# Attention steps of a two-layer block laid out anew: who holds which PSUM bank, and which engine splits what

## What is computed

```
h = layernorm(x) * (1 + ca) + sa
x = x + ga * attention_1(h)      # 32 heads of 64, 8 key heads, rotary, a window of 128, sinks
h = layernorm(x) * (1 + cb) + sb
x = x + gb * block_2(h)          # h + causal attention of rmsnorm(h), then a top-2 mixture of 8 experts
```

## Time and profile before

| | us |
|---|---|
| runs: median (lowest to highest, 3) | 1406.89 (1406.08 to 1414.29) |
| profiled execution, whole | 1400.63 |
| its span, first to last instruction | 1398.7 |
| TensorE busy in the span | 1064.0 (76%) |
| VectorE | 792.3 (57%) |
| ScalarE | 712.4 (51%) |
| GpSimd | 478.8 (34%) |

### The profile page before, as it was taken

One profiled execution on the slowest core, in us unless ns is written; L12 is line 12 of the kernel. 1 busy time (PEld: TensorE's weight loads), 2 busy tenths in 40 slices (PEclk: granted clock), 3 DMA queues, 4 the chain that ended last, 5 costly groups with the idle time before them and its releaser, 6 DMA issues.

```text
span 1398.7 us, 22967 instructions
## 1 busy us (share of the span) xinstructions
PE 1064.0 (76%) x6836; PEld 946.2 (68%) x6836; DVE 792.3 (57%) x2276; ACT 712.4 (51%) x2003; POOL 478.8 (34%) x659
## 2 busy tenths in 40 slices
PE   3647767777775677779878999988899726889893
PEld 1336666667665566668767888877788616888883
DVE  4445565555555554456655666656666553666655
ACT  2124535455453454566665666675676523555541
POOL 2355544755653454244222424322222140000003
PEclk7778978999997798999999999999999957999997
DMA  6455445545731343454344345534332063555513
GB/s 144 124 121 166 129 128 140 164 131 163 168 93 46 98 123 96 132 135 142 89 123 99 99 121 135 145 84 128 84 88 49 1 227 105 155 144 151 151 39 104
DMA packets 151823, 166.58 MB, mean 119 GB/s; under 512 B 79572, under 2 KB 108180, under 8 KB 146580
## 3 DMA queue, kind: packets, MB, share of 16 engines
q1 hardware_dynamic: 129427, 143.27, 38.8%
q10 hardware_dynamic: 20736, 17.64, 3.9%
q0 software_dynamic: 1536, 4.20, 0.9%
HBM read 106.28 MB, written 58.79 MB: 118 GB/s over the span
## 4 chain that ended last, share of the span: by engine, by line
PE 37%; issue 8%; DVE 6%; ACT 4%; DMA 3%; POOL 2%; ACTq 1%; SPq 0%; DVEq 0%; POOLq 0%
PE psO L917 7%; PE psS L882 5%; PE psX L892 4%; PE psP L817 4%; PE psS L1075 3%; PE psX L1075 3%; PE psY L933 3%; DMA kd<-st 2%; PE psO L1096 2%; PE psP L1096 2%; ACT pTh L1136 1%; DVE pbuf L1481 1%; PE psP L900 1%; DVE pTl L1497 1%; POOL xg L766 1%
## 5 line engine op out<-in xcount | busy, mean ns | idle before, releaser
L1167 ACT ACTIVATE pbuf<-pbuf,nmax 128x256 f32<-128x256 f32 (+3 forms) x512 | 265.5, 519 | 298.0 <-DVE nmax L1481 296.7
L1481 DVE CUSTOM_DVE_ANT_0 pbuf<-psS,mcau 128x256 f32<-128x256 f32 (+3 forms) x512 | 215.4, 437 | 55.8 <-PE psS L882 52.4
L1497 DVE TENSOR_TENSOR pTl<-psX,pTh 128x512 fp32r<-128x512 f32 x272 | 187.5, 689 | 76.0 <-ACT pTh L1136 73.4
L882 PE MATMUL psS<-kT,qE 128*128 128x256 f32 (+3 forms) x1024 | 214.6, 320 | 11.2 <-DVE nmax L1481 10.9
L687 POOL TENSOR_TENSOR ol<-oS,oh 128x256 fp32r<-128x256 f32 x128 | 94.7, 740 | 332.9 <-ACT oh L1136 332.7
L917 PE MATMUL psO<-pTh,vpad 128*128 128x256 f32 x1088 | 192.4, 300 | 13.5 <-DVE oS L1503 6.4
L1136 ACT ACTIVATE pTh<-psX 128x512 fp32r<-128x512 f32 x272 | 159.6, 587 | 51.0 <-PE psO L917 48.7
L882 PEld LDWEIGHTS psS<-kT,qE 128*128 128x128 f32 x1024 | 157.3, 202 | 24.4 <-DVE nmax L1481 22.1
L917 PEld LDWEIGHTS psO<-pTh,vpad 128*128 128x128 f32 x1088 | 151.9, 193 | 27.5 <-DVE pTl L1497 15.8
L892 PE MATMUL psX<-idn,pbuf 128*128 128x128 f32 x1088 | 169.8, 280 | 0.8 <-DVE pTl L1497 0.4
L892 PEld LDWEIGHTS psX<-idn,pbuf 128*128 128x128 f32 x1088 | 131.2, 144 | 6.8 <-DVE pTl L1497 1.6
(11 more groups left out here) (225 smaller groups left out, 2465.7 us busy)
## 6 DMA issues: line engine op xcount, KB each, us to landing
qd<-st SPq DMA_DIRECT2D x32, 1024.0 KB, 4.3
qE<-qd SPq DMA_DIRECT2D x128, 256.0 KB, 5.7
mrawV<-in_w_moe SPq DMA_DIRECT2D x32, 384.0 KB, 3.3
mrawB<-in_w_moe SPq DMA_DIRECT2D x32, 384.0 KB, 3.4
kT<-kd SPq DMA_DIRECT2D x64, 128.0 KB, 2.9
kT<-kd SPq DMA_DIRECT2D x32, 256.0 KB, 4.1
kd<-st SPq DMA_DIRECT2D x7, 1024.0 KB, 8.2
xg<-sq ACTq DMA_DIRECT2D x7, 640.0 KB, 3.4
```

What stands on the lines that cost most here:

```text
L882: last = mm(psS[j % 2][:, 0:n], qE[:, g % 2, j, t * P:(t + 1) * P], kT[:, g % 2, c, k0:k0 + n], start=(c == 0), stop=(c == 1))
L1167: nc.scalar.activation(pj, pj, ACT.Exp, bias=nmax[:, u % 4, j:j + 1], scale=-1.0, accum_out=sums[:, u % 4, j:j + 1]).then_inc(a_exp, 1)
L1481: V.tensor_tensor_reduce(probs(u, j), psS[j % 2][:, 0:n], mcau[:, SEQ - n:], -SCALE, 3e38, ALU.add, ALU.min, nmax[:, u % 4, j:j + 1]).then ...
L1497: V.tensor_tensor(pTl[:, kt % 2, :], psX[kt % 2][:, :], pTh[:, kt % 2, :], ALU.subtract).then_inc(v_pl, 1)
```

## The change

- `turn_scale` writes the right half of psO instead of psP, runs a step later (u-3) and right after the last values of that step; `scale_of` reads it there. The waits a_rx in `begin_item` and BANKED fall.
- In windowed steps the projection becomes the last thing TensorE does, and VectorE takes the item at the head of its next step. `denominator`, `out_hi` and `out_project` move a step later; the orders within all steps are new; TensorE and GpSimd run NU + 5 steps.
- All weight highs (80 copies of 128x512) and the highs of the rotated q and k (38) go from GpSimd to ScalarE; a weight high stands at the head of ScalarE's step. GpSimd keeps the lows. `sink_in` goes from GpSimd to VectorE.
- Features are turned in pairs of tiles, through a whole psP bank, as items of `ahead` at steps 15 and 18 of a segment; `turned` falls.
- SP's order of loads, stores and placements is new, with one list for windowed and one for causal steps.

The diff, cut to its core:

```diff
 def ahead(u):
+    if u % SEGU in (15, 18):
+        return ("f", 2 * (u // SEGU + 1) + (u % SEGU == 18), 0)
...
+            def step_window(u):        # SP
+                if m == 0:
+                    if quad:
+                        store_q(g + 1)
+                        place_k(g + 1)
+                        place_q(g + 1)
+                    else:
+                        place_k(1)
+                if m == 2:
+                    load_wq(g + 4)
+                if m == 3:
+                    load_wo(g + 1)
+                if m == 4:
+                    load_wkv(quad + 2, 0)
+                    store_q(g + 2)
+                    place(g + 2)
...
+                if m == 12:
+                    place_k(g + 4)
+                    load_wkv(quad + 2, 1)
+                if m == 13:
+                    store_q(g + 4)
+                    place_q(g + 4)
+                if m == 14:
+                    load_wq(g + 7)
+                if m == 15:
+                    load_wo(g + 4)
...
             def step(u):               # GpSimd
-                if 0 <= u - 1 < 2 * SEGU:
-                    sink_in(u - 1)
                 if 0 <= u - 4 < NU:
                     out_low(u - 4)
-                if 0 <= u - 2 < NU:
-                    spread(u - 2)
...
+                if turns(u - 1):
+                    rope_low(ahead(u - 1)[:2])
                 if u < NU:
+                    low_weights(u)
+                if turns(u):
+                    rope_sum(ahead(u)[:2])
+                if 0 <= u - 1 < NU:
+                    spread(u - 1)
...
             def turn_scale(u):
                 pe.wait_ge(g_rx, u + 1)
-                pe.wait_ge(v_pj, BANKED[min(u + 1, NU - 1)])
-                wait(pe, a_rx, u)
                 for i in range(2):
-                    last = turn(psP[:, i * P:(i + 1) * P], rdenx[:, i * P:(i + 1) * P], idn[:, :])
+                    last = turn(psO[:, (2 + i) * P:(3 + i) * P], rdenx[:, i * P:(i + 1) * P], idn[:, :])
...
             def step_window(u):        # TensorE, as it is after
+                scores(u, 0)
+                if nk > 0:
+                    turn_probs(u - 2, 0)
+                if u >= 3 and keys(u - 3) > 1:
+                    values(u - 3, 0)
+                if nk > 1:
+                    turn_probs(u - 2, 1)
+                if u >= 3:
+                    values(u - 3, keys(u - 3) - 1)
+                scores(u, 1)
+                if u >= 3:
+                    turn_scale(u - 3)
+                scores(u, 2)
+                if u >= 5:
+                    out_project(u - 5)
+                scores(u, 3)
+                if ahead(u):
+                    project(ahead(u))
...
             def step_window(u):        # ScalarE, as it is after
+                high_weights(u)
                 if nk > 0:
                     probs_hi(u - 2, 0)
                 exp_head(u, 0)
+                if u >= 3:
+                    scale_of(u - 3)
                 if nk > 1:
                     probs_hi(u - 2, 1)
+                if u >= 4:
+                    out_hi(u - 4)
                 exp_head(u, 1)
+                exp_head(u, 2)
                 if item and by_scalar(item):
                     high(item)
+                if u >= 1:
+                    sink_exp(u - 1)
+                if turns(u - 1):
+                    rope_high(ahead(u - 1)[:2])
                 exp_head(u, 3)
...
             def step_window(u):        # VectorE, as it is after
+                if u >= 1 and ahead(u - 1):
+                    take(ahead(u - 1))
                 mask_max(u, 0)
+                if u >= 2:
+                    denominator(u - 2)
                 mask_max(u, 1)
+                mask_max(u, 2)
                 if nk > 0:
                     probs_lo(u - 2, 0)
+                if u >= 1:
+                    sink_in(u - 1)
                 if u >= 3:
                     scale_out(u - 3)
                 if nk > 1:
                     probs_lo(u - 2, 1)
                 mask_max(u, 3)
                 between(u)
```

More of the change, by code:

```diff
@@ L144, with turns @@
 count_items()
-BANKED = []
-for _u in range(NU):
-    _n = BANKED[-1] if BANKED else sum(1 for _ in prologue_items())
-    BANKED.append(_n + (1 if ahead(_u) else 0) + len(turned(_u)))
 WPAIRS = [k for k in PAIR if not by_scalar((k[0], k[1], 0)) and k != ("k", 0)]
 TURN = {k: n + 1 for n, k in enumerate(WPAIRS)}
+def turns(u):
+    return 0 <= u < NU and ahead(u) is not None and ahead(u)[2] == 1 and ahead(u)[:2] in TURN
 def build(nc, x, w_attn, wo_attn, b_attn, outb, sinks, w_ffn, wo_ffn, ln1, ln2, gate, w_moe,
@@ L1183, in scale_of @@
                 wait(act, v_os, u - 1)
-                copy(rS[:, u % 2, :], psP[:, 0:2 * P]).then_inc(a_rx, 1)
+                copy(rS[:, u % 2, :], psO[:, 2 * P:4 * P]).then_inc(a_rx, 1)
             def out_hi(u):
@@ L1303, in _ @@
             root(0, None)
-            for t in range(TB):
-                high(("f", t, 0))
+            high_wq(0)
+            high_wkv(0, 0)
+            for n in range(2):
+                high(("f", n, 0))
+            high_wkv(0, 1)
             for i, dst in ((0, cosT), (1, sinT)):
@@ L1577, in step_window @@
                 between(u)
-                for n in turned(u):
-                    low(("f", n, 0))
             def step_causal(u):
                 now = u < NU
-                item = ahead(u) if now else None
                 nk = keys(u - 2) if u - 2 < NU else 0
+                if now and ahead(u - 1):
+                    take(ahead(u - 1))
+                if u - 3 < NU and keys(u - 3) > 3:
+                    probs_lo(u - 3, 3)
                 if now:
                     mask_max(u, 0)
-                if u - 1 < NU:
-                    denominator(u - 1)
-                if now:
                     mask_max(u, 1)
```

438 lines of the change are left out of this document (218 added, 220 removed).

## The result

The changed kernel takes 1149.62 us (median of 4 runs, 1145.55 to 1150.46) against 1408.51 (4 runs, 1406.08 to 1414.29): a ratio of 0.8151, 95% interval 0.8119 to 0.8184. The forecast was 1168, its range 1120 to 1240.

A forecast was written before the change was run, and what follows sets the result against it. One bank shared by reciprocals and projection was taken to hold TensorE, then VectorE, in windowed steps. Windowed 369 plus causal 412 make 781 against 1016, 235 less with 0.5 for the ends; span 1164, forecast 1168 us, range 1120 to 1240.

The forecast's parts named there:

- The bound: Windowed steps: bank shared by reciprocals and projection holds TensorE, then VectorE; 1.90 us of silence, 3.83 us of wait.
- The floor of TensorE and the windowed sum: Ordinary windowed quad: TensorE floor 77.6 us, x1.10 gives 85; four of them plus 29 make 369 us.
- The causal sum: Ordinary causal quad: floor 95.6 us, x1.07 gives 102; three, plus 16, plus 90 for the last make 412 us.
- ScalarE's highs: 80 weight and 38 rotation highs on ScalarE: 69 us, lower end 50; no path cost while loads are there.
- The slack of the loads: SP's queue issues each load two steps or more early; the tightest placement has some 8 us of slack.
- The sink sum: Moved to VectorE 64 times at den's mean of 0.395 us: 25 us in all; ends 0 and 1.22 us each.
- The rival that was built on it, 1209: VectorE's den and sink sum each meet GpSimd's rotation sums in 34 rotating steps: 41 us more; 12%.
- The ends: Outside the quads: prologue gains about 1 us, extra drain step costs 1.5; 0.5 us counted, bounds -4 and +5.
- DMA (1188): Same bytes in 85 us quads make DMA share 0.80; placements come late, perhaps 10 us a quad; 8%.
- Half the gain by the two score banks (1314): Score banks pace the loop: windowed steps 6.6 us instead of 5.3, +83; causal ones stay as they are, +63; 12%.
- The ring through ScalarE, GpSimd and SP (1410 to 1440): High, GpSimd's low, SP's load, landing, next high close a ring four steps long, 13 us of 21; 3%.
- The signs: Windowed quads 80 to 90 us, clock 0.97 or more, psP wait under 0.5, ScalarE 69 busier, GpSimd 70 to 90 less.

The follow-up runs named there:

- run 1: Kernel before, old order, with reciprocals turned into the free half of psO a step later and no projection wait for their copy: 1272.61 us.
- Run 10: Changed kernel with the highs of both the weights and the rotations back on GpSimd, new order kept: 1145.05 us.
- run 7: Changed kernel with the queue's old order of loads, stores and placements: 1150.6 us.
- run 6: Changed kernel with the sink sum back on GpSimd, at the head of its step: 1147.84 us.
- run 2: Kernel before with reciprocals in psO a step later and, on top, features turned in pairs as items at steps 15 and 18: 1262.68 us.
- run 8: Changed kernel with only the weights' highs back on GpSimd, each just ahead of its low: 1135.79 us.
- run 4: Changed kernel with the windowed projection back ahead of out-projection and heads 2 and 3, taken by VectorE in the same step: 1200.48 us.
- run 5: Changed kernel with the reciprocals back in psP and the projection waiting for their copy, new order kept: 1155.53 us.
- run 9: Changed kernel with only the rotations' highs back on GpSimd: 1145.54 us.

## Why the prediction was right, point by point

**The bound.** That one bank with two tenants held TensorE and then VectorE is right as a description of the old step; run 1 takes 101 us out of its windowed half (541.4 to 440.0), less whatever of that is the delay of the reciprocals. But the forecast gave the silence to the bank, and the runs give it to bank and order in such a way that they can't be added. In the old order bank and delay are worth 135 us of attention; in the new order the bank is worth 16. The new order with the old bank is worth 253 of the 259 us of the whole time, 248 of 263 in attention. In the windowed steps what fits both is that more work stands between the reciprocals and the projection. In the causal ones less stands there than before and the cost still fell, from 33 us to 13; what the delay and the other engines' orders have of that is open. The chain of waits, which the forecast took to say the same, covers only the span behind 513 us and so says nothing of the second quad.

**The floor of TensorE and the windowed sum.** 369 was forecast, 361.6 measured. Two ordinary quads at 85 each: they take 82.5 and 87.3, mean 84.9, so the x1.10 over 77.6 was right. The dear ones were to take 14 and 15 more; they take 94.8 and 97.0, so 10 and 12 more. The first of them has the late first exponential in it and a clock of 0.89, so its 10 are not normalizations and chains alone.

**The causal sum** is the term that was mis-sized most: 412 forecast, 391.3 measured. The ordinary quad took 98.8 us, x1.03 over the floor of 95.6 and not x1.07, and the extras for normalizations and chains, 9 and 7 us, measured 2.5 and 1.8: where TensorE is the bound with 97% and more of the quad, VectorE's extra work lies in VectorE's own idle. In the third quad, where VectorE is busy 86.7 us of 97.0, it comes through: TensorE waits 8.4 us there for nmax, 0.4 in the second quad. That is read off; no run takes the normalizations out.

**ScalarE's highs.** 69 us by the row of pTh; 71.4 measured. ScalarE's busy time grew by only 37.3 us (712.4 to 749.7), so the forecast sign "about 69 us busier" was wrong. Run 10, which has all highs back on GpSimd, shows 695.5 us: so the highs are worth 54.2 by busy time, and 16.9 us went elsewhere in the change. That 71.4 us of copies make 54.2 fits with rows in which a ScalarE instruction begins while the one before still runs (82.25 and 0.62 long, the next at 82.77); this is read off, not tested. GpSimd lost 75.2 (478.8 to 403.6), inside 70 to 90. The price on the path was put at nothing "while the loads are there". Over the quads that holds (8 to 10 change their sum by at most 2.4 us). At one place the load was not there, ahead of the very first exponentials, 13.9 us, of which 5.7 us of the load lie on the chain that ended last; the forecast worked out the slack of a quad in its stride and not that of the first one.

**The slack of the loads.** Behind that first one no weight high waits for its load, and the placed q lands in 5.8 us at a DMA share of 0.78 and 0.86 (0.80 was forecast). One high waits 5.6 us for the store out of st, that of a projected q at 396.2. With the old queue order three highs of wkv do wait and the windowed half is 6 us longer, though the time of run 7 is the same.

**The sink sum.** 25 us forecast on VectorE; 19.6 for the sum itself and 6.7 more for den (0.500 us in place of 0.395), so 26.3. At 229.80 a den takes 0.16 us, at 235.13, beside GpSimd's rotation sum from 235.03 on, 1.20. This agrees with the Trainium skill ("SBUF — State Buffer", Who interferes with whom): a VectorE instruction with two SBUF inputs contends with a GpSimd instruction that reads SBUF. It doesn't decide the time: without the sink sum on VectorE the kernel takes 1147.84 us (run 6). The rival that was built on it, 1209, fell: the second quad takes 82.5 us with VectorE busy 72.9 of them.

**The features.** No number was given to them alone except through the extras; they are worth 8 to 10 us in the old order (run 2).

**The ends.** 0.5 us forecast, 12.4 measured. The prologue is 2.4 us longer, not 1 shorter (between runs with the very same prologue it differs by 3.3 us, see run 8), and what follows the last mask 10.0 us longer (302.9 to 312.9), not 1.5. The drain itself is as it was (71.9 us from the last mask to the first relu before, 72.6 after). 8.0 us lie in the expert loop (204.8 to 212.8), which the change doesn't touch, and 1.3 behind it.

**The rivals.** DMA (1188): transfers were dense, and beyond the first high's load and one store nothing came late. Half the gain by the two score banks (1314): false in the new order, but the mechanism is real; run 4 brings it back at 54 us in the windowed steps. The ring through ScalarE, GpSimd and SP (1410 to 1440): its one link that showed is that first high. That nothing moves: fell.

**The signs.** The ordinary windowed quads lie between 80 and 90 us and GpSimd's loss in its range. The clock is 1.00 in the second quad but 0.96 in the third and fourth, where 0.97 was wanted, and VectorE's wait for psP is 1.3 us where 0.5 was; the windowed sum is right all the same.

**The number.** The forecast's 18 us too many are thus 7 windowed, 21 causal, minus 12 for the ends; 2 are the median against the span. That attention came out 28 us below and the ends 12 above is luck for the number. The last step of the sum isn't what its words say: 1166 and 6 are 1172, and 1168 adds 2. Measured, the median stands 0.1 us above the profiled execution.

## What to carry to other kernels

Ask of a bank with two tenants not who shares it but what stands between the two uses in the queues: with two heads and an out-projection in between, the sharing cost 3 us in 64 steps, with four transposes and a head 13, and a bank of its own in the old order won only half of what the new order won. When an engine reads a result, put that reading where its producer has long been done, and behind nothing on which a bank's release depends: one taking, moved ahead of oS, cost 82 us. And where the bound engine is truly full, extra work on the others cost about 2 us a quad; where two engines are nearly full, count it.

## What was not expected of the hardware

The expert loop runs the same instructions in every kernel here, and took from 203.1 (run 5) to 212.8 us (changed kernel), 204.8 in the kernel before. Stretches of 26 us in it, changed kernel and then the kernel before:

```profile
942.00:968.00 26.00, 23.37 (x148) 22.56 (x148) 16.08 (x28) 13.00 (x26) 0.00 (x0) 0.93 0.49 138
...
1072.00:1098.00 26.00, 23.19 (x158) 22.41 (x157) 16.54 (x28) 14.04 (x28) 0.00 (x0) 1.00 0.13 43
```

```profile
1207.00:1233.00 26.00, 23.15 (x157) 22.38 (x156) 16.48 (x29) 13.98 (x29) 0.00 (x0) 1.00 0.53 149
```

TensorE is as busy in the one as in the other (23.4 and 23.2 of 26 us) but the clock is 0.93 in the first, a mixture of its two levels, 2.4 and 1.2 GHz: the trace has short pieces at the lower one, five within the changed kernel's loop, four in those of runs 6 and 7 (210.8 and 207.7 us), two in that of the kernel before, none in run 1's (205.0), one in run 5's. Fewer matmuls begin in such a stretch, 148 against 157. Over the whole loop the clock is 0.95 in the changed kernel and 0.98 before; 0.95 of 212.8 us is 202.2 and 0.98 of 204.8 is 200.7, 1.5 apart where the loops are 8.0 apart, so by this estimate the clock makes most of the 8 us. It is not all: run 9's loop has two such pieces and a clock of 0.97, and took 210.4. The Trainium skill ("TensorE: Matmul & The Clock Gate", HAM oscillation — how this bites in real kernels) tells of such swings in loops in which TensorE waits for transfers. Here it doesn't: its waits in the changed kernel's loop are for VectorE's hTl, 21.6 us, and 19.3 before. No run here tells why the clock falls in some kernels and not in others, with the same loop. All this makes some 8 us of this case's tail a property of neither version of the attention, and a difference of under 1% between two kernels here is to be read with that in mind: those of runs 5 and 8 to 10 from the changed kernel above all.
